# A graph network's last node phase: root rows made in the third node phase, one batch at a time, gate multiplied on ScalarE

## The reference, cut to what matters

```python
q, k, v = x @ Wq + bq, x @ Wk + bk, x @ Wv + bv      # 4 heads of 32
p = exp(score(q[dst], k[src]) - max over the edges of dst)
out = segment_sum(v[src] * p / denom[dst], dst)      # N x 128
x_r = x @ Wskip + bskip                              # the root rows
beta = sigmoid(concat([out, x_r, out - x_r]) @ Wbeta)
x = layernorm(x + beta * x_r + (1 - beta) * out)
```

## Time and profile before

| | |
|---|---|
| time, median of 3 runs | 5381.8 us (5381.48, 5381.8, 5394.01) |
| profiled execution: its own time, and its span | 5392.99 us, 5391.3 us |
| mean granted clock of TensorE | 0.675 of full speed |
| busy, share of the span: PE, PEld, DVE, ACT, POOL | 65%, 50%, 65%, 29%, 73% |
| third node phase (N2) | 4047.4 to 4177.2 us |
| attention over the edges (L3) | 4177.2 to 5266 us |
| last node phase (N3) | 5268.1 to 5391.3 us |

### The profile page before, as it was taken

One profiled execution on the slowest core, in us unless ns is written; L12 is line 12 of the kernel. 1 busy time (PEld: TensorE's weight loads), 2 busy tenths in 40 slices (PEclk: granted clock), 3 DMA queues, 4 the chain that ended last, 5 costly groups with the idle time before them and its releaser, 6 DMA issues. The chain is left out here.

```text
span 5391.3 us, 85535 instructions
## 1 busy us (share of the span) xinstructions
PE 3515.6 (65%) x19081; PEld 2691.1 (50%) x19081; DVE 3509.0 (65%) x6976; ACT 1541.4 (29%) x3619; POOL 3954.8 (73%) x4526
## 2 busy tenths in 40 slices
PE   4444444356666666556888888866663688888873
PEld 3333333244444444344666666655552566666662
DVE  6555322238878888635777777778884566666667
ACT  1111111142222222232222222267773122222222
POOL 7777777677777777647777777678877777777763
PEclk7555565578888888765555555578886677777775
DMA  7555565536667777516666666678984667776761
GB/s 234 184 184 186 180 186 180 156 101 201 206 209 210 208 208 207 151 56 158 171 170 170 170 171 169 155 243 288 293 286 124 203 212 213 215 215 214 213 186 49
DMA packets 804058, 1015.33 MB, mean 188 GB/s; under 512 B 230872, under 2 KB 509411, under 8 KB 803942
## 3 DMA queue, kind: packets, MB, share of 16 engines
q1 hardware_dynamic: 454164, 466.36, 28.6%
q0 software_dynamic: 144320, 323.10, 23.2%
q10 hardware_dynamic: 205458, 224.65, 11.8%
HBM read 652.07 MB, written 361.61 MB: 188 GB/s over the span
## 5 line engine op out<-in xcount | busy, mean ns | idle before, releaser
L523 POOL DMA_INDIRECT L_gath<-tab,src x832 | 797.1, 958 | 256.5 <-issue 252.8
L523 POOL DMA_INDIRECT L_gath<-in_x,src x832 | 788.0, 947 | 259.1 <-issue 249.5
L523 POOL DMA_INDIRECT L2a_gath<-tab_h,src x832 | 790.1, 950 | 253.9 <-issue 253.9
L523 POOL DMA_INDIRECT L_gath<-tab_kv,src x832 | 789.4, 949 | 253.7 <-issue 237.6
L658 ACT ACTIVATE L_back<-L_pB 128x512 f32<-128x512 f32 x624 | 364.8, 585 | 896.9 <-PE L_pB L629 888.6
L641 DVE TENSOR_TENSOR_SCAN L_acc<-L_mask,L_acc,L_pT 128x512 f32<-128x512 bf16 x207 | 264.8, 1279 | 537.0 <-PE L_pT L587 536.2
L587 PE MATMUL L_pT<-ident,L_gath 128*128 128x128 f32 x832 | 222.5, 420 | 533.6 <-DMA L_gath<-in_x,src 529.7
L629 PE MATMUL L_pB<-ident,L_acc 128*128 128x128 f32 x2496 | 522.1, 349 | 0.9 <-DVE L_acc L772 0.5
L718 POOL TENSOR_SCALAR L_hoth<-L_row,L_high,ew_sb 128x49 f32<-128x49 bf16 x832 | 442.9, 560 | 67.1 <-DVE L_part L760 65.2
L629 PEld LDWEIGHTS L_pB<-ident,L_acc 128*128 128x128 f32 x2496 | 410.5, 184 | 156.3 <-issue 153.0
L587 PEld LDWEIGHTS L_pT<-ident,L_gath 128*128 128x128 f32 x832 | 143.8, 210 | 609.4 <-DMA L_gath<-in_x,src 478.9
(11 more groups left out here) (287 smaller groups left out, 7642.5 us busy)
## 6 DMA issues: line engine op xcount, KB each, us to landing
run<-L_back ACTq DMA_DIRECT2D x416, 256.0 KB
L_seed<-seed SPq DMA_DIRECT2D x416, 256.0 KB, 3.6
run<-L_back ACTq DMA_DIRECT2D x208, 264.0 KB, 2.6
seed<-L_zeros SPq DMA_DIRECT2D x208, 256.0 KB, 3.9
sent<-L2a_gath ACTq DMA_DIRECT2D x208, 256.0 KB, 2.8
L_sent<-sent SPq DMA_DIRECT2D x208, 256.0 KB
run<-L_back SPq DMA_DIRECT2D x208, 256.0 KB, 4.8
L_mask<-same SPq DMA_DIRECT2D x208, 128.0 KB, 3.2
```

The source lines that it names most:

```text
L523: gp.indirect_dma_start(out=gath[k][:, t, :], out_offset=None, in_=table, in_offset=bass.IndirectOffsetOnAxis(ap=g["src"][:, tile:tile + 1 ...
```

## The change

The root rows x_r are made in N2: TensorE gets a stage `root_rows` at lag 7 into the PSUM banks pA and pU, which N2 did not use, and VectorE a stage `keep_root` at lag 8 that adds the bias (now a broadcast tile `wide["bskip"]`) and writes the result over the batch's `xT`. At the start of the attention phase VectorE reduces all 49 tiles of root rows with `w_skip` to `g["skip_dot"]`. The last phase has no matmuls; its `steps` go batch by batch with lags 0, 1 and 2; the dot product starts from `skip_dot`; ScalarE computes both the gate and its complement by Sigmoid and multiplies the root rows with the gate (L1676 is an existing instruction of that form), and VectorE adds x and the sums times the complement. The three-part bias in the setup is gone, and one broadcast load is there in its place.

```diff
 class Setup:
-        self.biases = [("bskip", "L3_gnn_bskip")]
+            (wide["bskip"][:, :], line(d["L3_gnn_bskip"]).to_broadcast([P, D])),
     def sync_rows(self, sp):
-        for j in range(3):
-            sp.wait_ge(self.s_part, j + 1)
-            sp.dma_start(g["bias"][j:j + 1, :], self.part[j][:, :]).then_inc(self.s_w, 16)
     def scalar_first(self, act, pX):
-        for name, source in self.biases:
-            first = at[name]
-            act.dma_start(self.bias[:, first:first + d[source].shape[0]], ...).then_inc(self.s_bias, 16)
     def vector_first(self, v):
-        v.memset(g["ones3"][:, :], 1.0)
-        v.wait_ge(self.s_bias, 16 * len(self.biases))
-        for j in range(3):
-            v.tensor_copy(self.part[j][:, :], self.bias[:, :]).then_inc(self.s_part, 1)
-            v.wait_ge(self.s_part, j + 1)
-            if j < 2:
-                link(v.tensor_tensor(self.bias[:, :], self.bias[:, :], self.part[j][:, :], ALU.subtract))
 def edges_attention(nc, d, g):
+            root_rows, beta_w = g["xT"].rearrange("p (t f) -> p t f", f=D), g["wide"]["beta"]
+            link(v.tensor_tensor(w_skip[:, :], beta_w[:, D:2 * D], beta_w[:, 2 * D:3 * D], ALU.subtract))
+            for n in range(NB):
+                for t in tiles_of(n):
+                    ins = v.tensor_tensor_reduce(junk[:, t - n * BT, :], root_rows[:, t, :], w_skip[:, :], 1.0, 0.0, ALU.mult, ALU.add, g["skip_dot"][:, t:t + 1])
+                link(ins)
             v.wait_ge(s_lane, 16)
 def nodes_on(nc, ph, g, layer, table, index):
+        def root_rows(n, k, r):
+            room(pe, s_kept, n, 2)
+            for t in range(count(n)):
+                m = pe.matmul((pA, pU)[n % 2][:, cols(t)], g["xT"][:, cols(n * BT + t)], w["Wskip"][:, :], start=True, stop=True)
+            m.then_inc(s_root, 1)
-                           2: [(3, turn_new), (4, tables)]}[layer])
+                           2: [(3, turn_new), (4, tables), (7, root_rows)]}[layer])
+        def keep_root(n, k, r):
+            need(v, s_root, n)
+            m = count(n)
+            v.tensor_tensor(own_rows[:, span(n), :], (pA, pU)[n % 2][:, 0:m * P].rearrange("p (t f) -> p t f", t=m), tiled(wide["bskip"][:, :], m),
+                            ALU.add).then_inc(s_kept, 1)
-                           2: [(1, gather_up), (2, turned), (4, keep_biased)]}[layer])
+                           2: [(1, gather_up), (2, turned), (4, keep_biased), (8, keep_root)]}[layer])
 def nodes_out(nc, ph, g, out, table, index):
     (VectorE)
-            for t in range(m):
-                a = v.tensor_tensor(sums[k][:, t, :]..., got[:, n * BT + t, 0:D]..., inv_den[:, t, :]..., ALU.mult)
-            need(v, s_y, n)
-            v.tensor_tensor(flow[k][:, 0:m, :], mine, sums[k][:, 0:m, :], ALU.subtract)
-            v.tensor_tensor(y[k][:, 0:m, :], sums[k][:, 0:m, :], g["x"][:, span(n), :], ALU.add)
-            for t in range(m):
-                link(v.tensor_tensor_reduce(junk[:, :], sums[k][:, t, :], w_out[:, :], 1.0, 0.0, ALU.mult, ALU.add, half[:, 0, t:t + 1]))
-                link(v.tensor_tensor_reduce(junk[:, :], pY[n % 2][:, cols(t)], w_skip[:, :], 1.0, 0.0, ALU.mult, ALU.add, half[:, 1, t:t + 1]))
-            v.tensor_tensor(dot[k][:, 0:m], half[:, 0, 0:m], half[:, 1, 0:m], ALU.add).then_inc(s_dot, 1)
+            link(v.tensor_tensor(sums[k][:, 0:m, :]..., got[:, span(n), 0:D]..., den..., ALU.mult))
+            for t in range(m):
+                a = v.tensor_tensor_reduce(junk[:, t, :], sums[k][:, t, :], w_out[:, :], 1.0, g["skip_dot"][:, n * BT + t:n * BT + t + 1],
+                                           ALU.mult, ALU.add, dot[k][:, t:t + 1])
+            a.then_inc(s_att, 1)
+
+        def mix(n, k, r):
+            m = count(n)
+            need(v, s_att, n)
+            need(v, s_part, n)
+            link(v.tensor_tensor(y[k][:, 0:m, :], y[k][:, 0:m, :], g["x"][:, span(n), :], ALU.add))
             for t in range(m):
-                a = v.scalar_tensor_tensor(y[k][:, t, :], flow[k][:, t, :], beta[k][:, t:t + 1], y[k][:, t, :], ALU.mult, ALU.add)
+                a = v.scalar_tensor_tensor(y[k][:, t, :], sums[k][:, t, :], rest[k][:, t:t + 1], y[k][:, t, :], ALU.mult, ALU.add)
...
+        steps(NB, BT, [(0, attend), (1, mix), (2, turned)])
     (ScalarE)
+        def gate(n, k, r):
+            need(act, s_att, n)
+            room(act, s_xn, n, BT)
+            m = count(n)
+            act.activation(beta[k][:, 0:m], dot[k][:, 0:m], ACT.Sigmoid).then_inc(s_go, 1)
+            act.activation(rest[k][:, 0:m], dot[k][:, 0:m], ACT.Sigmoid, scale=-1.0)
+            need(act, s_go, n)
+            for t in range(m):
+                a = act.activation(y[k][:, t, :], root_rows[:, n * BT + t, :], ACT.Copy, scale=beta[k][:, t:t + 1])
+            a.then_inc(s_part, 1)
...
+        steps(NB, BT, [(0, gate), (1, root), (2, norm)])
```

More of the change, by code:

```diff
@@ L220, in __init__ @@
         self.far = [ph.sb(f"far{j}", [P, TILES], BF16) for j in range(2)]
-        bias_all = g["bias"].shape[1]
-        self.bias = ph.sb("bias", [1, bias_all])
-        self.part = [ph.sb(f"part{j}", [1, bias_all], BF16) for j in range(3)]
         self.src, self.low, self.same8 = ph.sb("src", [P, TILES], I32), ph.sb("low", [P, TILES], BF16), ph.sb("same8", [P, TILES], U8)
@@ L228, in __init__ @@
         self.halves = [ph.sb(f"half{j}", [P, TILES], BF16) for j in range(2)]
-        (self.s_src, self.s_dst, self.s_w, self.s_x, self.s_same, self.s_id, self.s_mask, self.s_tp, self.s_tc, self.s_link, self.s_bias, self.s_part,
-         self.s_rim, self.s_open) = (ph.sem(n) for n in ("src", "dst", "w", "x", "same", "id", "mask", "tp", "tc", "slink", "bias", "part", "rim", "open"))
+        (self.s_src, self.s_dst, self.s_w, self.s_x, self.s_same, self.s_id, self.s_mask, self.s_tp, self.s_tc, self.s_link,
+         self.s_rim, self.s_open) = (ph.sem(n) for n in ("src", "dst", "w", "x", "same", "id", "mask", "tp", "tc", "slink", "rim", "open"))
         w, wide = g["w"], g["wide"]
@@ L1111, in edges_attention @@
         rim, den = slot("rim", [GT, 2, W3]), slot("den", [GT, 2, D])
+        w_skip, junk = ph.sb("w_skip", [P, D]), ph.sb("junk", [P, BT, D])
         state, fixed = slot("state", [P, 4, GT + 1]), slot("fixed", [P, 2, GT])
@@ L1502, in nodes_on @@
     (s_go, s_gz, s_agg, s_turn, s_aT, s_u, s_uT, s_y, s_sum, s_var, s_std, s_inv, s_xn, s_turnx, s_xnT, s_tab, s_comb, s_link, s_eps, s_part,
-     s_pad, s_cgo, s_pre, s_plus, s_own) = (ph.sem(n) for n in ("go", "gz", "agg", "turn", "aT", "u", "uT", "y", "sum", "var", "std", "inv", "xn", "turnx", "xnT", "tab",
-                                         "comb", "link", "eps", "part", "pad", "cgo", "pre", "plus", "own"))
+     s_pad, s_cgo, s_pre, s_plus, s_own, s_root, s_kept) = (ph.sem(n) for n in ("go", "gz", "agg", "turn", "aT", "u", "uT", "y", "sum", "var", "std", "inv", "xn", "turnx", "xnT", "tab",
+                                         "comb", "link", "eps", "part", "pad", "cgo", "pre", "plus", "own", "root", "kept"))
     s_got = ph.slot_sems("got", NB)
@@ L1748, in _ @@
         sp.wait_ge(s_out, 16 * parts)
-    @block.tensor
-    def _(pe):
-        at = g["bias_at"]["bskip"]
-        def skip(n, k, r):
-            room(pe, s_dot, n, 2)
-            for t in range(count(n)):
-                pe.matmul(pY[n % 2][:, cols(t)], g["xT"][:, cols(n * BT + t)], w["Wskip"][:, :], start=True, stop=False)
-                m = pe.matmul(pY[n % 2][:, cols(t)], g["ones3"][:, :], g["bias"][:, at:at + D], start=False, stop=True)
-            m.then_inc(s_y, 1)
-        steps(NB, 2, [(0, skip)])
     @block.vector
@@ L1800, in mix, with turned, root, norm @@
             need(v, s_var, n)
-        def turned(n):
-            inverse(v, n, ring(n), link, mv, std, inv, off, s_std, s_inv)
-        for j in range(len(groups) + 2):
-            for n in groups[j - 2] if j >= 2 else ():
-                turned(n)
-            for n in groups[j] if j < len(groups) else ():
-                if n >= 2 * GN:
-                    need(v, s_xn, n - 2 * GN)
-                attend(n)
-            for n in groups[j - 1] if 1 <= j <= len(groups) else ():
-                mix(n)
+        def turned(n, k, r):
+            inverse(v, n, k, link, mv, std, inv, off, s_std, s_inv)
+        steps(NB, BT, [(0, attend), (1, mix), (2, turned)])
     @block.scalar
     def _(act):
-        act.wait_ge(s_eps, 1)
-        for j in range(len(groups) + 2):
-            for n in groups[j - 2] if j >= 2 else ():
-                normed(act, g, n, ring(n), y, inv, off, s_inv, s_xn)
-            for n in groups[j] if j < len(groups) else ():
-                need(act, s_dot, n)
-                act.activation(beta[ring(n)][:, 0:count(n)], dot[ring(n)][:, 0:count(n)], ACT.Sigmoid).then_inc(s_beta, 1)
-            for n in groups[j - 1] if 1 <= j <= len(groups) else ():
-                root_of(act, n, ring(n), mv, std, eps, s_var, s_std)
+        def gate(n, k, r):
+            need(act, s_att, n)
```

(10 more changed lines are left out.)

57 lines of the change are left out of this document (19 added, 38 removed).

## The result

| | before | after |
|---|---|---|
| time, median | 5385.5 us (5381.48 to 5394.01, 5 runs) | 5354.78 us (5351.95 to 5356.93, 5 runs) |
| profiled execution, span | 5391.3 us | 5351.7 us |
| third node phase | 130.4 us | 129.1 us |
| attention over the edges | 1090.9 us | 1085.0 us |
| last node phase | 123.1 us | 91.8 us |

The account below looks back on a forecast made before the run. GpSimd's queue was taken to set the third node phase and attention, VectorE the last node phase. Last phase -28.7 and setup +0.5 give -28.2 us, from the median 5381.8 to 5354 us; range 5345 to 5369.

Parts of the forecast that it names:

- VectorE binds before, 8.48 us a batch: Last node phase before the change: VectorE sets the time, with attend 5.70, mix 2.50 and closing pair 0.28 us.
- 6.25 us a batch after: Last node phase after: VectorE's step of attend 2.74, mix 3.22 and closing pair 0.28 us, bounds 6.1 to 6.6.
- ScalarE 6.1 us, nearly level with VectorE: Last node phase after: ScalarE's step of gate, root and norms with two table loads takes 6.1 us, against VectorE's 6.25.
- Rival (2): Last phase: a table switch costs as much again as its load, ScalarE's step 8.7 us, 5382 us, no difference; chance 0.04.
- The third node phase: 0: Third node phase: added root products and additions cost nothing, under 28 us of cover from GpSimd's scatters.
- Rival (4): Third node phase: added pairs reach past the last scatter, +4 to +9 us, 5360 us, still faster; chance 0.05.
- The attention: 0: Attention's start: 49 reductions take 16.2 us on VectorE, some 3 us show, absorbed in three batches, cost 0.
- Rival (1): Attention: reductions hold GpSimd's issue or its late start isn't absorbed, up to 16 us back, 5370, no difference; chance 0.07.
- The setup: +0.5: Setup: one more broadcast load on ScalarE ahead of evicting the turned x, +0 to +1.4 us, taken as +0.5.
- Rival (3): Last phase: each batch's mix and norms wait in line, step 12.4 us, +33 us, 5415 us, slower; chance 0.04.
- The sum, -28.2: Whole kernel: -28.7 us from the last phase and +0.5 from the setup, other phases 0.

## Why the prediction was right, point by point

**VectorE binds before, 8.48 us a batch.** Right: 8.47 to 8.50 with the same instructions in another order. In the kernel before itself VectorE also waits for ScalarE, 0.9 us twice for the norms of an earlier group and 4.9 us at the end for the root; the prediction names no such wait, and has it only in the sentence that the end is shorter.

**6.25 us a batch after.** 6.03 to 6.09, 6.05 in the mean. The mechanism held, the term was a little too large. Mix and the closing pair are as added up (5304.55 to 5307.77 is 3.22, then 0.29). Attend is 2.52 (5302.03 to 5304.55) for 2.74: the four reductions take 1.09, not 1.32. Each is 0.35 long and starts 0.27 after the one before, less than the lower end of 0.29 that the prediction had from grouped rows. Ten full steps make 2.0 us of the 2.7 by which the phase is shorter than forecast (91.8 for 94.5).

**ScalarE 6.1 us, nearly level with VectorE.** 5.98 where it is alone the bound. It turned out to be a tie within 0.06 us, closer than the error of either term (6.25 for 6.03, 6.1 for 5.98), so that VectorE binds and not ScalarE is right with some luck. That the switch has no drain beside its load, on which the forecast hung, is what the rows of after show too: 23 of the 24 loads start within 0.02 us of the end of the work ahead, and the first stands behind a wait for VectorE. Rival (2) is refuted by them and by the run without switches. The load's price by the Trainium skill, page "ScalarE: Activation LUTs", section "What ACT_TABLE_LOAD costs", is that of the rows (1283 ns); its 1380 ns of drain appears in no row here, and where page and measurement differ the measurement decides. Loads were 24, not 26: the first two gates follow each other, and so do the last two roots (the one at 5345.03 has no load), so each pair shares one.

**The third node phase: 0.** Right, VectorE 73.30 for 74, TensorE 61.54 for at most 100, the last kept rows at 4148.2 with scatters to 4172.4. The phase without them is as long (129.5 for 129.1 and 129.8). Rival (4) falls.

**The attention: 0.** The result right, two of its numbers too large: the reductions take 12.2 us and not 16.2, since those without a link between them overlap more than the ones in the last phase (0.22 us from start to start), and the first comparison is not 3 us late but not late at all. Rival (1) falls on both its halves. Its late start is covered up to about 27 us. And none of the fetches beside the 49 reductions of 128x128 is lengthened (0.90 to 0.97 us). Where the prediction has one addition a batch hold GpSimd now, it misreads the rows: of the last phase's 49 fetches before, the one at 5277.48 is the only one above 1.02 us.
The Trainium skill's rule that a VectorE operation with two SBUF inputs locks the shared port (page "SBUF — State Buffer", section "SBUF: two separate sides") agrees with the 128x512 operations (1.36 for 0.95); with these reductions, which have two SBUF inputs too, no fetch shows it.

**The setup: +0.5.** The copies of the turned x start with their load at 38.05 us. The same place was at 37.42 before: +0.6. GpSimd's gathers, which run through that phase, don't carry it on: the last one starts at 1047.21 for 1048.73 before.

**Rival (3), hand-overs in line.** Falls: VectorE waits 0.7 us in the phase after its second batch.

The sum, -28.2, stands against -30.7 of the medians, and the last phase alone, -31.4 for -28.7, accounts for the difference. That is as far as the account can go: the interval of the ratio leaves 26 to 37 us, and the two profiled executions differ by 39.5, 5.9 of it in the attention and 2.2 ahead of it. That 5354 was forecast and 5354.78 measured is in part luck: the change gave 2.5 us more than forecast, and the median of before, 5381.8 over the first three runs, came out at 5385.5 over five.

## What to carry to other kernels

When work moves from a full engine to an idle one, add up both to the tenth of a microsecond: here the receiver filled up exactly, and the next saving on VectorE alone is worth 0.06 us a batch and one on ScalarE alone 0.02 at most, while one on both brought 0.7. A period read from one engine over a few batches can hide that the other falls behind; read both from the same instruction to itself. And to know how much more can be laid beside a bound queue, multiply what lies there until the queue waits: four times the reductions showed some 27 us of cover.

## What the runs showed of the hardware that was not expected

A table load doesn't stand behind the wait of the instruction that needs it (but for the first of a phase): it starts within 0.02 us of the end of the work ahead, though the operand comes 0.8 us later. A hold of GpSimd by VectorE hits a fetch that starts inside a longer VectorE operation, in either form of instruction at 128x512 (1.36 for 0.94), in a row of scalar-tensor-tensors of 128x128 (1.42) and in a conversion with one operand (1.33); beside the 128x512 ones the fetch then ends 0.82 us after the operation does. Reductions of 128x128 don't hold a fetch and are themselves lengthened by it (0.35 for 0.29). Reductions that follow each other without a semaphore start 0.22 us apart at a length of 0.29, and 0.27 at 0.35 in the last phase, where their start value comes from memory. And one chip ran the same kernel in 6684 to 6765 us (medians) that another ran in 5386 to 5389, with the same time for the VectorE and ScalarE instructions compared (0.69 and 1.28).
